# Full attention with q and k in two float32r halves on two 64-row tiles instead of three bf16 parts

## The reference, cut to what matters

```python
q = (hidden_states @ Wq.T + bq).reshape(b, s, HEADS, HEAD_DIM)
k = (hidden_states @ Wk.T + bk).reshape(b, s, HEADS, HEAD_DIM)
v = (hidden_states @ Wv.T + bv).reshape(b, s, HEADS, HEAD_DIM)
q = q * SCALE
scores = jnp.einsum('bqhd,bkhd->bhqk', q, k)
probs = jax.nn.softmax(scores.astype(jnp.float32), axis=-1).astype(scores.dtype)
out = jnp.einsum('bhqk,bkhd->bqhd', probs, v).reshape(b, s, d)
return out @ Wo.T + bo
```

## Time and profile before

| | |
|---|---|
| time, median of 3 runs | 2994.47 us (2993.47 to 2994.68) |
| span of the profiled execution | 3043.6 us |
| PE busy | 2495.8 us (82%) |
| DVE busy | 2292.3 us (75%) |
| ACT busy | 1887.0 us (62%) |
| POOL busy | 1220.7 us (40%) |
| L1350, maxima on DVE | 601.9 us, 512 of 1219 ns |
| L1323, exponentials on ACT | 556.3 us, 1024 of 601 ns |
| L1257, second scores on PE | 293.6 us, 387 ns |
| L1267, prob by v on PE | 281.3 us, 621 ns |

### The profile page before, as it was taken

How to read it: one execution, slowest core, us unless ns; L and a number is a source line. 1 busy time by engine, 2 the same in 40 slices (tenths; PEclk the granted TensorE clock), 3 DMA queues, 4 the chain that set the end, 5 groups by cost and what they waited for, 6 DMA issues and landing times. The chain is left out here.

```text
span 3043.6 us, 43434 instructions
## 1 busy us (share of the span) xinstructions
PE 2495.8 (82%) x13082; PEld 1107.6 (36%) x13254; DVE 2292.3 (75%) x4236; ACT 1887.0 (62%) x3760; POOL 1220.7 (40%) x1394
## 2 busy tenths in 40 slices
PE   6897899999998899969999999895746555565666
PEld 5543222222222444424444444485711111111466
DVE  7777888888888477866666666665369999999843
ACT  2213688888887421326666666414459999999743
POOL 2015434433335101638888888704522020200054
PEclk8999899999999999979999999997879999989678
DMA  4002322222233100732222222463221111110122
GB/s 100 1 1 89 93 74 74 74 74 75 74 114 103 45 1 1 257 128 88 87 82 84 85 87 92 140 202 79 56 76 42 43 43 43 45 40 31 46 67 75
DMA packets 193925, 229.11 MB, mean 75 GB/s; under 512 B 55824, under 2 KB 122128, under 8 KB 193248
## 3 DMA queue, kind: packets, MB, share of 16 engines
q1 hardware_dynamic: 158960, 193.15, 20.0%
q0 software_dynamic: 31360, 30.05, 4.0%
q10 hardware_dynamic: 3376, 3.15, 0.4%
HBM read 139.72 MB, written 87.95 MB: 75 GB/s over the span
## 5 line engine op out<-in xcount | busy, mean ns | idle before, releaser
L1350 DVE TENSOR_REDUCE neg_max<-ps 128x1 f32<-128x1024 f32 x512 | 601.9, 1219 | 99.8 <-PE ps L1243 92.1
L1323 ACT ACTIVATE prob<-ps 128x512 f32<-128x512 f32 x1024 | 556.3, 601 | 95.3 <-PE ps L1257 82.1
L2650 DVE TENSOR_REDUCE neg_max<-ps 128x1 f32<-128x1024 f32 x512 | 581.2, 1210 | 13.4 <-PE ps L2444 13.2
L2520 ACT ACTIVATE ps<-ps,neg_max 128x1024 f32<-128x1024 f32 x512 | 557.3, 1089 | 23.0 <-DVE neg_max L2650 22.1
L1530 POOL TENSOR_TENSOR acc<-acc,prob 128x512 f32<-128x512 f32 (+3 forms) x320 | 535.3, 1692 | 64.5 <-PE ps L1624 31.3
L1779 DVE CUSTOM_DVE_ANT_0 ps<-ps,mask_strip 128x512 f32<-128x512 f32 (+7 forms) x512 | 382.4, 776 | 221.7 <-PE ps L1598 221.7
L2444 PE MATMUL ps<-k_stack,q_stack 128*128 128x512 bf16 x1000 | 328.6, 414 | 240.9 <-ACT ps L2520 219.1
L1738 ACT ACTIVATE prob<-ps 128x512 f32<-128x512 f32 (+3 forms) x640 | 270.4, 474 | 210.0 <-PE ps L1612 149.7
L1257 PE MATMUL ps<-q_stack,k_stack 128*128 128x512 bf16 x946 | 293.6, 387 | 12.2 <-DMA k_low<-k_parts 5.1
L1267 PE MATMUL ps<-prob,v 128*32 128x512 f32 x2048 | 281.3, 621 | 3.7 <-ACT prob L1323 0.7
L2444 PEld LDWEIGHTS ps<-k_stack,q_stack 128*128 128x128 bf16 x1024 | 62.4, 99 | 502.2 <-ACT ps L2520 424.2
(11 more groups left out here) (368 smaller groups left out, 3944.2 us busy)
## 6 DMA issues: line engine op xcount, KB each, us to landing
q_stack<-q_parts SPq DMA_DIRECT2D x576, 48.0 KB
k_stack<-k_parts SPq DMA_DIRECT2D x576, 48.0 KB
o_quads<-o_out SPq DMA_DIRECT2D x64, 256.0 KB
v<-v_wide SPq DMA_DIRECT2D x32, 512.0 KB
o_pairs<-o_out SPq DMA_DIRECT2D x64, 256.0 KB
num<-o_pairs SPq DMA_DIRECT2D x8, 2048.0 KB, 8.7
q_parts<-parts SPq DMA_DIRECT2D x24, 384.0 KB, 2.5
k_parts<-parts SPq DMA_DIRECT2D x24, 384.0 KB, 2.7
```

Of the source, the lines that this page charges most:

```text
L1323: nc.scalar.activation(prob[:, m % RING, :], ps[:, bank(m), :], ACT.Exp).then_inc(exped.sem, 1)
L1350: nc.vector.tensor_reduce(neg_max[:, i.slot(2), m:m + 1], ps[:, first:first + 2, :].rearrange("p b n -> p (b n)"), AX.X, ALU.max, negate=T ...
L2520: nc.scalar.activation(s, s, ACT.Exp, bias=neg_max[:, n % 2, qt:qt + 1], accum_out=sums[:, cols(n * KTS + qt, 1)]).then_inc(summed.sem, 1)
L2650: nc.vector.tensor_reduce(neg_max[:, n % 2, qt:qt + 1], ps[:, first:first + 2, :], AX.XY, ALU.max, negate=True).then_inc(maxed.sem, 1)
```

## The change

In this layer alone q and k are split in two parts and not three. [...] A product is now four products of parts: 4 x 8 = 32 rows (`PRODUCTS`). All matmuls of scores read them as float32r.

The stacks are float32 and hold two tiles of 64 rows each (`TILE_ROWS`): q's 32 rows stand at row 0 and again at row 64, with the two rows of the shift behind each. k's keys 0 to 511 stand on the first tile and keys 512 to 1023 on the second, so that `k_stack` is half as long. `load_halves` fills one tile with three DMAs on SP, so six per head and one for v. `q_low`, `k_low` and POOL's loads are gone, and so are the memsets of `q_stack`. First-pass pairs run as before on both halves of the array. Second scores, which used the whole array, now use one half each, and the order of tiles is changed so that they alternate between the halves. The shift is split into float32r numbers, turned by a float32r matmul by an identity (`ident_r`, made once by POOL at the program's start) and written by two DMAs.

In PE's order the first pair of a group's first scores moves ahead of prob by v; the second stays behind the fourth second score.

```diff
-                nc.scalar.activation(parts[:, s, n, 0, :], z[:, s, n, :], ACT.Copy).then_inc(hi_ready.sem, 1)
+                if halved:
+                    nc.scalar.activation(upper[:, s, n, :].bitcast(F32R), z[:, s, n, :], ACT.Copy).then_inc(hi_ready.sem, 1)
+                else:
+                    nc.scalar.activation(parts[:, s, n, 0, :], z[:, s, n, :], ACT.Copy).then_inc(hi_ready.sem, 1)
...
+    def subtract_upper(eng, g, s):
+        for n in (0, 1):
+            hi_ready.wait(eng, g * 2 + n)
+            eng.tensor_tensor(z[:, s, n, :], z[:, s, n, :], upper[:, s, n, :], ALU.subtract).then_inc(lo_ready[n].sem, 1)
...
+def load_halves(sp, S, b, h, t, q_rows, k_rows, keys, loaded):
+
+    q = S.q_halves[b:b + 1, h, :, :, :].rearrange("b a d t -> b (a d) t")
+    sp.dma_start(q_rows[t * TILE_ROWS:t * TILE_ROWS + PRODUCTS, :],
+                 q.broadcast_to([2, 2 * HD, SEQ])).then_inc(loaded, 16)
+    for a in (0, 1):
+        first = t * TILE_ROWS + a * 2 * HD
+        k = S.k_halves[b:b + 1, h, a, :, keys]
+        sp.dma_start(k_rows[first:first + 2 * HD, :],
+                     k.broadcast_to([2, HD, k.shape[-1]])).then_inc(loaded, 16)
...
-    tiles = [(kt, c) for kt in range(KTS) for c in range(CH)]
+    tiles = [(g, half, c) for g in range(KTS // 2) for c in range(CH) for half in (0, 1)]
...
-                nc.tensor.matmul(ps[:, first, :], q[own, m * P:(m + 1) * P], k[own, 0:GROUP], start=True, stop=True)
-                nc.tensor.matmul(ps[:, first + 1, :], q_low[i.slot(2)][low, m * P:(m + 1) * P],
-                                 k_low[i.slot(2)][low, :], start=True, stop=True).then_inc(s1_mm.sem, 1)
+                for half in (0, 1):
+                    rows = slice(half * TILE_ROWS, half * TILE_ROWS + PRODUCTS)
+                    op = nc.tensor.matmul(ps[:, first + half, :], q[rows, m * P:(m + 1) * P].bitcast(F32R),
+                                          k[rows, :].bitcast(F32R), start=True, stop=True)
+                op.then_inc(s1_mm.sem, 1)
...
-                nc.tensor.matmul(ps[:, bank(n), :], ks[j.slot(4)][:, kt * P:(kt + 1) * P],
-                                 qs[j.slot(4)][:, c * GROUP:(c + 1) * GROUP], start=True,
+                nc.tensor.matmul(ps[:, bank(n), :], ks[j.slot(4)][rows, g * P:(g + 1) * P].bitcast(F32R),
+                                 qs[j.slot(4)][rows, c * GROUP:(c + 1) * GROUP].bitcast(F32R), start=True,
                                  stop=True).then_inc(s2_mm.sem, 1)
...
                         for m in range(4 * g, 4 * g + 3):
                             second_scores(j, m, there(n, 1))
+                    if one:
+                        first_pass(i, 2 * g)
                     if g > 0 and two:
                         weigh(j, g - 1)
...
                     if two:
                         second_scores(j, 4 * g + 3, there(n, 1))
                     if one:
-                        first_pass(i, 2 * g)
                         first_pass(i, 2 * g + 1)
...
-                    sp.dma_start(qs[h.slot(4)][STACK:STACK + SHIFT, :].rearrange("r (q t) -> r q t", t=P),
-                                 shift_rows[0:SHIFT * KTS, h.slot(2), :]).then_inc(shifted[h.slot(2)], 16)
+                    for first in (PRODUCTS, TILE_ROWS + PRODUCTS):
+                        sp.dma_start(qs[h.slot(4)][first:first + SHIFT, :].rearrange("r (q t) -> r q t", t=P),
+                                     shift_rows[0:SHIFT * KTS, h.slot(2), :]).then_inc(shifted[h.slot(2)], 16)
```

More of the change, by code:

```diff
@@ L1264, in weigh @@
                 exped.wait(pe, j.times(NT, 4 * g + 3))
-                for n, (kt, c) in enumerate(groups[g], 4 * g):
-                    quad = (c * 2 + kt % 2) * 32
-                    nc.tensor.matmul(ps[quad:quad + VW, OB, :], vs[j.slot(4)][:, :, kt], prob[:, n % RING, :],
-                                     start=kt < 2, stop=kt >= KTS - 2).then_inc(pv_mm.sem, 1)
+                for n, (_, half, c) in enumerate(groups[g], 4 * g):
+                    quad = (c * 2 + half) * 32
+                    nc.tensor.matmul(ps[quad:quad + VW, OB, :], vs[j.slot(4)][:, :, g + half * KTS // 2],
+                                     prob[:, n % RING, :], start=g == 0, stop=g == KTS // 2 - 1).then_inc(pv_mm.sem, 1)
             def turn_shift(h, j):
```

97 lines of the change are left out of this document (46 added, 51 removed).

## The result

The changed kernel takes 3622.11 us (median of 4 runs, 3616.74 to 3623.02), the kernel before 2993.97 us beside it (4 runs, 2991.35 to 2994.68). The ratio is 1.2096 with a 95% interval of 1.2079 to 1.2114: 628 us slower, where 35 were forecast, and far outside the range. The profiled execution spans 3620.4 us.

A forecast was written before the change was run, and what follows sets the result against it. A 2.43 us ring through ACT, almost level with TensorE and DVE, was taken to bind. Sum: 58 heads x 0.73 = +42.3, last two heads +1.5, late load -4, projection -4.8; +35 on 2994.5 gives 3029 us, range 2976 to 3060.

The forecast's parts named there:

- the lower clock: Full attention: idle TensorE might lose the granted 1.00; given no case, as the causal stage keeps 0.93 at 43 of 76 busy.
- item 1: Float32r scores on two 64-row tiles take one stream, step 0.216; TensorE's work per group falls from 2.64 to about 2.1 us.
- item 2: Four-byte weight loads exposed at the fourth and third scores, 0.095 us each: 0.19 per group.
- E: Rival: float32r scores take two streams; group path 3.46, head 14.0, 3184 us in all; chance 0.09.
- A: Rival: weight loads hidden at both the fourth and third scores; 2.65 per group, head 10.76, 2984 us; chance 0.19.
- B: Rival: one of the two score weight loads hidden; head 11.14, +12, 3006 us; chance 0.15.
- Item 3: New order: a first-score pair between third score and prob by v adds 0.22 us per group.
- The ring: Fourth score, ACT's exponential, released third score, prob by v, next fourth score: 2.43 us per group before, 2.84 after.
- C: Rival: halved matmul work wins and DVE sets the pace; head about 9.9, -62, 2932 us; chance 0.10.
- The 2.43: Path through ACT per group before the change: 1.08 to the released third score, 0.32 to prob by v, 1.03 to fourth.
- Item 5: Six DMAs per head leave POOL's queue, ending a 4.24 us TensorE wait for a late k_low load: -4 us.
- Item 7: Projection: less POOL work speeds DVE's normalization, 0.95 us less per group over five groups: -4.8 us, between 0 and -6.

The follow-up runs named there:

- the unsteady version: Changed kernel with second scores on all 64 rows of each tile (zeros in q), first scores kept on 32: 3194.89, 3477.25, 3612.86 and 3617.94 us.
- the 64-row version: Changed kernel with all scores over the 64 rows of their tiles, the added rows zeros in q: 3042.79 us, one execution.
- the 64-row version in the old order: Changed kernel with all scores over 64 rows and both pairs of first scores behind the group's fourth score again: 3016.24 us, ratio 1.0082.

## Why the prediction was wrong

**The failed step is the sentence that gave the lower clock no case, and so put its price at nothing.** The rivals' paragraph named it ("the stage might lose the granted 1.00") and dismissed it because the causal stage keeps 0.93 with TensorE busy for 43 of 76 us. The comparison was with the wrong quantity. It took the share of busy time for what the clock follows, so that a stage could be without it only by being idle. The stage ran at 0.50 with 291 busy us of 291. It began at 0.50, as the kernel before does, and didn't get the clock back. What the change took away was rows: the scores of the kernel before use 128 rows of the array in each second score and 64 in each of a pair of first scores, those of the changed kernel 34 and 32 of 64. No row of before shows such narrow scores on both passes, so none could have shown that this matters, and none excluded it. An unseen condition deserved a chance and a price, and the price could be worked out: TensorE's 2.1 us of item 1 twice over are 4.2 a group against 10.79 / 4 = 2.70, over 256 groups 384 us more, some 3380 us in all without the forms of tile (an estimate, which takes a step at 0.50 for twice one at 1.00; prob by v was measured at 1.87 and 1.03). The traces show the clock going down over waits (5.76 us in the kernel before, 8.78 in the changed one, 4.62 in the unsteady version), in one version also in mid-work (bf16, second scores on 34 rows, at 998 us, with TensorE busy for 7.40 of the 8 us ahead), and not coming back with it recorded as busy: 0.50 with 1317.85 us busy of 1320.

**The part that was not in the sum at all** is the change of form between 32 and 34 rows. Item 1 counted on neighbours on different tiles streaming side by side, and item 2 put the fourth score "on another tile shape" than prob by v, but took both kinds of score for one shape. That is 0.21 us a group at a granted clock of 1.00 and 170 us of this result at 0.50. It doesn't decide the outcome: without it the result is still 3452 us.

How the 628 us divide, by the chain of versions from the changed kernel back: 3622 to 3452 (one form of tile) 170; to 3043 (64 rows, upper clock) 409; to 3016 (old order) 27; to 2992 (bf16 in three parts) 24; 630 in all, since they were measured on several chips. The first two are not independent: at the upper clock the forms would cost about 54.

**What held.** With the clock restored, the 64-row version takes 3042.79 us against the forecast of 3029 (its head 11.78 against 11.52, which over 63 heads is 16 us), and its group can be laid on the forecast step by step:

```profile
605.79 0.50 PE L1276 MATMUL ps<-q_stack,k_stack 64*128 64x512 f32 x1
...
606.98 0.50 PE L1276 MATMUL ps<-q_stack,k_stack 64*128 64x512 f32 x2 [0.26 <-ACT prob L1342]
...
607.64 1.10 PE L1286 MATMUL ps<-prob,v 128*32 128x512 f32 x8
...
608.66 0.49 PE L1276 MATMUL ps<-q_stack,k_stack 64*128 64x512 f32 x1
```

- Item 1, one stream: right. No row of before shows the price of a float32r product, and one stream was the author's choice between its two bounds. At 1.00 a score alone takes 0.49 to 0.50 (387 + 105), never the 592 of a float32 instruction; E is out.
- Item 2, loads exposed at both places: right. Fourth score to the released one: 606.98 - 605.79 = 1.19 (forecast 1.17). A and B are out.
- Item 3, released score to prob by v: 0.66 (0.63), prob by v 1.02 (1.03). The ring is 2.87 (2.84).
- C is out: DVE is busy for 242.56 of 291 us at 1.00, and no version is faster than the kernel before by more than 2 us.
- The ring fits the whole and not its halves, and that is in part luck. By the same sum either half alone should have been nearly free (2.65 and 2.62 against the 2.64 of before), and they cost 0.58 and 0.44 a head. The 2.43 left out the third score in groups 0 and 2, which costs 0.22 on one tile and little on two; the pair's price in bf16 is 0.32 and not 0.22; and in the old order the second pair meets DVE.
- Item 5, the late load, -4: wrong, and hidden here only by the slow heads. At the upper clock the wait is still there, with no load of `k_low` left to blame. In the 64-row version in the old order on the timeline:

```profile
998.89 1.34 SPq L1424 DMA_DIRECT2D q_stack<-shift_rows  x2
...
1008.32 1.19 PE L1276 MATMUL ps<-q_stack,k_stack 64*128 64x512 f32 x3 [4.28 <-issue]
```

And the DMA view of 990 to 1010 us (busy tenths of the DMA engines in 0.5 us steps):

```profile
DMA  1111020111118999899999997221111111111111
```

Six loads of 256 KB of sums, issued on POOL from 994.71, keep the DMA engines at eight or nine tenths from 996 to 1002 and land after 8.9 us (median). The shift's two DMAs go out at 998.89, in the middle of it, and the next head's second scores start at 1008.32 after 4.28 us of idle time. The stall is there without any load on POOL's queue behind the sums, so moving the loads off that queue doesn't end it; the transfers themselves are what is left in common. That the shift is what arrives last is likely from the order of the issues, and no row names it.
- Item 7, the projection: right in kind and under-estimated. Its period (the rows answer to the earlier trace rows):

```profile
266.36 2.17 DVE L196 TENSOR_SCALAR xn<-x_res,mean,rstd 128x128 f32<-128x128 f32 x4
...
271.11 2.18 DVE L196 TENSOR_SCALAR xn<-x_res,mean,rstd 128x128 f32<-128x128 f32 x4
```

271.11 - 266.36 = 4.75 us against 6.24; 5.3 was forecast. Four tiles take 2.17, no more than the 2.3 of mostly undisturbed ones, which fits POOL no longer disturbing them; no version separates it. First scores start at 301.73 (302.5 forecast, 307.26 before). Of these 5.5 us 2.0 are left at the first copy of the shift, because the second head's scores now wait longer for their loads: SP's issue at 301.46 lasts 5.08 us, and TensorE stands for 6.09 before 316.46, where it stood for 1.84 before.

## What to carry to other kernels

Before a matmul is made narrower (a smaller contraction on a smaller tile), read the granted clock of the stage and ask what holds it: here both passes on 34 of 64 rows cost 409 us with the engine nearly never idle, and filling up to 64 rows with zeros gave it back. Look too at where the clock was lost: a wait ahead of the stage had taken it in every version (0.50 from 310 to 325 us), and only those with at least one wide pass got it back at once (0.95 to 1.00 from 335 to 340). Give operations that alternate one form of tile: 32 and 34 rows are not one (5.19 us a group with both, 4.50 with 34 alone, at 0.50). And a ring that explains a period doesn't price an edit alone: sum it for every group, not for one, and where three limits lie within 0.2 us, undo each half on the chip before adding them up.

## What the runs showed of the hardware

- The granted clock can stay at 0.50 while TensorE is recorded as busy (1317.85 of 1320 us), and be 1.00 for the same instructions over more rows, even if one operand's added rows are zeros (3452 against 3043 us; in bf16 3470 against 2987 to 2994).
- It also fell in mid-work, after the last wide first scores (992.30): in bf16 with second scores on 34 rows it goes to 0.50 at 998 us, and with 128 rows the same tail keeps 1.00 (11.47 and 10.01 us busy of 12).
- In between there is an unsteady place: one kernel gave 3195 to 3618 us, rose in mid-stage with no change in its work, and was back at 0.50 after a wait of 4.62 us.
- A float32r matmul of 512 columns over 64 rows at 1.00: a step of 0.21 us (three on two tiles in 0.70) against 0.216 in bf16, 0.49 us alone, its weight load 183 ns against 96, about 0.1 of it exposed behind a wait or a change of form (0.49 against 0.387 alone). At 0.50 the load takes 283 ns over 32 rows and 294 over 34.
- Scores on 34 rows and on 64 have one form (in the version with first 34, second 64 both start at 607.71); 32 rows have another (0.72 us between starts at 0.50, 0.43 at 1.00).
